# Local attention in a decoder layer: scores of both head groups in PSUM banks of their own, and every engine's order re-dealt

## The reference, cut to what matters

```python
qkv = shift_tokens(x) @ Wqkv                 # 128 -> 3 x 1024, 16 heads of 64
q, k = l2norm(q) * qs, l2norm(k) * ksc       # then rotary tables on both
sim  = q @ k(window and the one before) * 8  # windows of 32 tokens, masked
out  = softmax(sim) @ v
x    = out @ Wo + x
h    = layernorm(shift_tokens(x))
x    = ((h @ W1a + b1a) * gelu(h @ W1g + b1g)) @ W2 + b2 + x
```

## Time and profile before

| | us |
|---|---|
| median of 3 runs | 2246.68 (2245.82 to 2247.02) |
| profiled execution, its own time | 2248.77 |
| span of that profile | 2247.0 |
| TensorE, share of the span busy | 94% |
| VectorE | 82% |
| ScalarE | 74% |
| GpSimd | 74% |

### The profile page before, as it was taken

The page is one execution under the profiler, slowest core; times in us unless marked ns, Lnnn a source line. Parts: engine busy times, 40 slices in busy tenths (PEclk is TensorE's granted clock), DMA queues, the critical chain, the costliest instruction groups (busy, mean ns, idle before and its releaser), DMA issues. The chain is left out here.

```text
span 2247.0 us, 70768 instructions
## 1 busy us (share of the span) xinstructions
PE 2105.5 (94%) x26387; PEld 1439.5 (64%) x26387; DVE 1842.6 (82%) x2689; ACT 1660.0 (74%) x3300; POOL 1654.5 (74%) x1553
## 2 busy tenths in 40 slices
PE   5899869999889999999999999999999999999995
PEld 3555436666646676667676676667667666676764
DVE  4898967777778888888888888888888888888883
ACT  5898845454368788788878878887887887888773
POOL 4677852333378888888888888888888888888881
PEclk8999999999999999999999999999999999999996
DMA  2222220000012223232322322232232222223221
GB/s 77 104 69 67 64 77 1 2 1 1 8 47 77 70 61 79 71 81 61 81 70 59 81 70 76 67 79 72 59 81 70 71 72 74 78 58 82 70 66 45
DMA packets 103501, 140.43 MB, mean 62 GB/s; under 512 B 63376, under 2 KB 64400, under 8 KB 103056
## 3 DMA queue, kind: packets, MB, share of 16 engines
q1 hardware_dynamic: 103440, 139.64, 23.0%
HBM read 56.39 MB, written 1.31 MB: 26 GB/s over the span
## 5 line engine op out<-in xcount | busy, mean ns | idle before, releaser
L1740 PE MATMUL f_psA<-f_W,f_xT 128*128 (+1 forms) x1154 | 603.4, 619 | 7.7 <-ACT f_Vt L1492 3.6
L1630 DVE TENSOR_TENSOR f_m<-f_psA,f_tab 128x1024 f32<-128x1024 f32 x385 | 460.0, 1215 | 78.5 <-ACT f_sq L1474 78.5
L1410 POOL TENSOR_TENSOR f_qkr<-f_qkr,f_rn 128x1024 f32<-128x1024 f32 x192 | 361.4, 1904 | 17.2 <-POOL f_rn L1433 17.2
L1381 POOL TENSOR_TENSOR f_Pr<-f_Pr,f_rden 128x384 f32<-128x384 f32 x384 | 308.1, 835 | 87.2 <-DVE f_rden L1619 87.2
L1474 ACT ACTIVATE f_sq<-f_psA 128x512 f32<-128x512 f32 x385 | 222.2, 590 | 107.0 <-PE f_psA L1740 103.5
L1740 PEld LDWEIGHTS f_psA<-f_W,f_xT 128*128 128x128 f32 x1154 | 192.6, 190 | 131.2 <-issue 90.5
L1606 DVE TENSOR_REDUCE f_mx<-f_psS 128x8 f32<-128x768 f32 x192 | 183.9, 958 | 83.6 <-PE f_psS L1775 83.6
L1400 POOL TENSOR_TENSOR f_qkr<-f_m 128x512 f32<-128x512 f32 x192 | 244.7, 1274 | 7.5 <-DVE f_m L1630 7.5
L1401 POOL TENSOR_TENSOR f_qkr<-f_m 128x512 f32<-128x512 f32 x192 | 246.4, 1283 | 0.0
L795 POOL TENSOR_TENSOR x_Es<-x_E 128x512 f32<-128x512 f32 x64 | 81.4, 1272 | 188.8 <-PE x_psO L1012 127.7
L1661 DVE TENSOR_REDUCE f_ssq<-f_sq 128x32 f32<-128x2048 f32 x96 | 218.5, 2276 | 0.0
(11 more groups left out here) (176 smaller groups left out, 4710.8 us busy)
## 6 DMA issues: line engine op xcount, KB each, us to landing
f_V<-f_Vt SPq DMA_DIRECT2D x96, 384.0 KB, 4.5
f_V<-f_Vt SPq DMA_DIRECT2D x96, 256.0 KB, 3.7
f_W<-in_f_W SPq DMA_DIRECT2D x48, 344.0 KB, 4.6
m_Cb<-m_BC_rows SPq DMA_DIRECT2D x64, 256.0 KB, 3.2
f_W<-in_f_W SPq DMA_DIRECT2D x48, 296.5 KB, 4.2
f_V<-f_Vt SPq DMA_DIRECT2D x48, 128.0 KB, 2.3
f_xsA<-xall SPq DMA_DIRECT2D x98, 32.0 KB
f_xsA<-xall SPq DMA_DIRECT2D x98, 31.8 KB
```

The costliest lines, as they stand in the source:

```text
L1381: pool.tensor_tensor(pv, pv, rv.unsqueeze(3).broadcast_to([P, 2, 2, KEYS]), ALU.mult).then_inc(Pr_ready[g][j], 1)
L1410: pool.tensor_tensor(qv, qv, rv.unsqueeze(3).broadcast_to([P, 2, GH, DH]), ALU.mult).then_inc(qkr_ready[g], 1)
L1630: dve.tensor_tensor(m12[:, j, :, half].rearrange("p m (h d) -> p m h d", d=DH), psA[n % 2][:, :].rearrange("p (h d) -> p h d", d=DH).unsqu ...
L1740: pe.matmul(psA[n % 2][:, :], xT[:, t, :], weights(i, W_QKV + n * 512, 512), start=True, stop=True).then_inc(A_full[n_fill], 1)
```

## The change

PSUM is dealt anew. `psD` is one bank, `psO` is gone, `psX` has two banks. Group 0's scores are in `psX`, group 1's in `psS`. Every tenant of every bank moves accordingly, with the waits that guard them. On TensorE both `scores` calls stand together, group 1 first, and the products with V of both groups behind them; the projection done ahead for the next tile is 2 and not 1; the three gates are in the D slot, at its end, and the three ups at the start of the E slot. ScalarE's, VectorE's, GpSimd's and SP's orders follow: all three GELUs are in the D slot between two table loads; ScalarE's exponentials come as 1, 0; V loads go in front of x1's shifted rows. No arithmetic is added or removed.

```diff
-        psD = [ps(f"f_psD{j}", [P, 512]) for j in range(2)]
+        psD = ps("f_psD", [P, 512])
...
-        psO = ps("f_psO", [P, 4, P])
-        S4 = psS[:, :, 0:GH // 2 * KEYS].rearrange("p a (c k) -> p a c k", k=KEYS)
+        psX = ps("f_psX", [P, 2, 512])
+        project_bank = [psP[:, :], psX[:, 0, :], psA[1][:, :], psA[0][:, :], psA[0][:, :], psA[1][:, :]]
+        S2 = [psX, psS]
+        S4 = [x[:, :, 0:GH // 2 * KEYS].rearrange("p a (c k) -> p a c k", k=KEYS) for x in S2]
...
         def probs_bank(g, half):
-            return psS[:, half, :] if g else (psO[:, :, :].rearrange("p c q -> p (c q)"), psP[:, :])[half]
+            return psX[:, half, :] if g else (psA[0][:, :], psD[:, :])[half]
...
         def qk_bank(g, half):
-            return psS[:, half, :] if g else (psP[:, :], psD[1][:, :])[half]
+            return psS[:, half, :] if g else (psD[:, :], psP[:, :])[half]
...
         def out_bank(g):
-            return psP[:, :].rearrange("p (c q) -> p c q", q=P) if g else psO[:, :, :]
+            return (psP, psA[0])[g][:, :].rearrange("p (c q) -> p c q", q=P)
...
+        def gate_bank(c):
+            return (psP[:, c * T2:(c + 1) * T2], 0) if c < 2 else (psD[:, T2:2 * T2], 1)
+        def a_bank(c):
+            return (psX[:, 1, c * T2:(c + 1) * T2], 0) if c < 2 else (psD[:, T2:2 * T2], 1)
```

SyncE, GpSimd and ScalarE (order inside a slot, new side; waits as before unless shown):

```diff
# SP: shift_in, then
+                if "E" in stages and not (isinstance(i, int) and i > ITERS):
+                    load_up_projection(i - 1)
+                if "A" in stages:
+                    for j in range(2):
+                        sp.wait_ge(A_free[8 + j], u + 1)
+                    for g in range(2):
+                        at_least(sp, O_free[g], u - 1)
+                    (V96 loads, Vtail first where t == 1)
                 if "C" in stages:
                     sp.wait_ge(x1_ready, i * 2 + (t - 1))
                     (xsC loads)
# POOL: rn, scale 1, scale 0, then
+                    normalise_probs(wu, 1, 0)
+                    normalise_probs(wu, 1, 1)
+                    residual_bias(done, i + (t - 2), q)
                     scaled_tables(u + 1, i + t, 1 - t)
-                    for g in range(2):
-                        normalise_probs(wu, g, 0)
-                        normalise_probs(wu, g, 1)
-                    rotate(u, t, 0)
-                    residual_bias(done, i + (t - 2), q)
+                    normalise_probs(wu, 0, 0)
+                    normalise_probs(wu, 0, 1)
                     rotate(u, t, 1)
+                    rotate(u, t, 0)
                     normalise_rows(done, i + (t - 2), q)
# ACT, whole slot, new order
+ square 3; evacuate_qk(1,0); square 2; evacuate_qk(0,1); evacuate_qk(0,0); square 1; evacuate_v(0)
+ evacuate_qk(1,1); square 0; evacuate_tokens; evacuate_probs (1,1) (1,0) (0,1) (0,0); evacuate_v(1)
+ lnq; rn0; lnC; rstdC; evacuate_out(1); evacuate_out(0); exponentials(1); D: xnT; exponentials(0)
+ D: preload GELU; gate_gelu(2); gate_gelu(0); gate_gelu(1); preload LN_EXP
# DVE, whole slot, new order
+ E: gated 0, 1, 2; table_products 3, 2; statistics; table_products 1, 0; squares' sum
+ maximum(1); less_maximum(1); maximum(0); less_maximum(0); denominators(1); x1
+ reciprocals(1); denominators(0); reciprocals(0); E: x2
```

TensorE, whole slot, new order with the waits that are new:

```diff
+ E: wait S_free[0]; up(0); up(1); wait ge_ready (first GELU); up(2)
+ wait x1_ready (slot before); project 3
+ transpose_qk(1)
+ (E: wait h2_ready, ge_ready; D: P_free[0][1], O_free[0] of the slot before) transpose_qk(0)
+ wait S_free[0]; D: wait x2_done; project 1
+ wait A_free[3]; project 4;  wait A_free[4]; transpose_tokens;  wait A_free[5]; project 0;  wait A_free[2]; project 5
+ (wait S_free[0], A_free[1], E: h01_ready) transpose_probs(1);  (wait A_free[8], xT_ready) transpose_probs(0)
-                    if g == 1:
-                        pe.wait_ge(S_free[0], v + 1)
-                    elif "C" in stages:
+                    if g == 0 and "C" in stages:
                         pe.wait_ge(P_free[1][0], wu + 1)
                         pe.wait_ge(P_free[1][1], wu + 1)
+ scores(1); scores(0)
+ (wait P_free[1][*], P_free[0][0]) times_v(1);  (wait P_free[0][*], A_free[0]) times_v(0)
+ wait A_free[9]; project 2 of the next tile
+ D: wait hatC_ready, O_free[0]; hatC transposes;  wait O_free[0], O_free[1]; W_O
+ E: wait S_free[0]; W_2
+ D: wait xnT_ready, w1_loaded, P_free[0][1]; gate(2); gate(0); gate(1)
```

More of the change, by code:

```diff
@@ L1334, in slot @@
                         sp.dma_start(xsC[0:1, 1, 64:D], x1[P - 1:P, 0, 64:D]).then_inc(xsC_ready[t], 16)
[L1335 to L1349, removed]
                 if "A" in stages and t == 1 and not is_first(i):
@@ L1486, in evacuate_v @@
                     act.wait_ge(A_full[8 + j], u + 1)
-                    if j == 1 and not is_first(i):
+                    if j == 0 and not is_first(i):
                         act.wait_ge(V96_ready[t], i * 32)
@@ L1516, in slot @@
                 if "A" in stages:
-                    square(u, 0)
                     square(u, 3)
@@ L1520, in slot @@
                     evacuate_qk(1, 0)
+                if "A" in stages:
+                    square(u, 2)
+                if "B" in stages:
+                    evacuate_qk(0, 1)
                     evacuate_qk(0, 0)
+                if "A" in stages:
+                    square(u, 1)
+                    evacuate_v(0)
+                if "B" in stages:
                     evacuate_qk(1, 1)
                 if "A" in stages:
-                    square(u, 2)
+                    square(u, 0)
                     evacuate_tokens(u + 1, 1 - t)
-                if "B" in stages:
-                    evacuate_qk(0, 1)
+                if "C" in stages:
+                    evacuate_probs(1, 1)
+                    evacuate_probs(1, 0)
+                    evacuate_probs(0, 1)
+                    evacuate_probs(0, 0)
                 if "A" in stages:
                     evacuate_v(1)
[L1530 to L1543, removed]
                     act.wait_ge(ssq_ready, u + 1)
                     act.activation(lnq[:, :], ssq[:, :], ACT.Ln, bias=consts[:, 0:1], scale=SSQ_SCALE).then_inc(lnq_done, 1)
-                    square(u + 1, 1)
+                    at_least(act, rn_ready, u)
+                    act.wait_ge(lnq_done, u + 1)
+                    act.activation(rn0[:, :], lnq[:, :], ACT.Exp, bias=consts[:, 1:2], scale=-0.5).then_inc(rn0_ready, 1)
                 if "c" in stages:
@@ L1574, in slot @@
                     gate_gelu(2)
+                    gate_gelu(0)
+                    gate_gelu(1)
+                    act.preload_act_table_set(LN_EXP)
+                if stages == "CcE":
+                    final_deviation(0)
             evacuate_tokens(0, 0)
-            square(0, 1)
             slot(0, 0, "A")
@@ L1726, in _ @@
             slot(ITERS + 1, 0, "cD")
+            final_rows(1)
             slot(ITERS + 1, 1, "E")
@@ L1768, in scores @@
                             r = slice(par * HQ, par * HQ + HQ)
-                            pe.matmul(S4[0:HQ, par, :, 0:WIN], same_row[r, 0:HQ], outside[r, :].rearrange("p (c k) -> p c k", k=WIN), start=False, stop=False, skip_group_check=True)
+                            pe.matmul(S4[g][0:HQ, par, :, 0:WIN], same_row[r, 0:HQ], outside[r, :].rearrange("p (c k) -> p c k", k=WIN), start=False, stop=False, skip_group_check=True)
                     for c in range(4):
@@ L1823, in transpose_qk @@
                     else:
-                        at_least(pe, O_free[1], v - 1)
-                        if t == 0 and not (isinstance(i, int) and i < 2):
-                            pe.wait_ge(h01_ready, (i - 1) * 2)
-                        at_least(pe, A_free[5], v)
+                        if "E" in stages:
+                            pe.wait_ge(h2_ready, i)
+                            pe.wait_ge(ge_ready, (i - 1) * 3)
+                        else:
+                            at_least(pe, P_free[0][1], wu)
+                            at_least(pe, O_free[0], wu)
+                        if isinstance(i, int) and "A" in stages:
+                            pe.wait_ge(A_free[0], u)
                     alone(pe, passed)
@@ L1836, in transpose_qk, with gate, up @@
                                 ins.then_inc(A_full[4 + 2 * g + half], 1)
-                def w1(n, c, full):
-                    ins = pe.matmul(bank_of(c)[0][0:FC[c], :], W1[:, n * FF + c * P:n * FF + c * P + FC[c]], xnT[:, :], start=True, stop=True)
+                def gate(c):
+                    ins = pe.matmul(gate_bank(c)[0][0:FC[c], :], W1[:, FF + c * P:FF + c * P + FC[c]], xnT[:, :], start=True, stop=True)
                     if c > 0:
-                        ins.then_inc(full[bank_of(c)[1]], 1)
+                        ins.then_inc(gate_full[gate_bank(c)[1]], 1)
+                def up(c):
+                    ins = pe.matmul(a_bank(c)[0][0:FC[c], :], W1[:, c * P:c * P + FC[c]], xnT[:, :], start=True, stop=True)
+                    if c > 0:
```

(23 more changed lines are left out.)

206 lines of the change are left out of this document (104 added, 102 removed).

## The result

The changed kernel takes 2221.78 us (median of 4 runs, 2220.61 to 2222.71), against 2246.25 us of the kernel before beside it: a ratio of 0.9892, 95% interval [0.9875, 0.9909], or 24.5 us less. The forecast was 2213, in a range of 2195 to 2250. The profiled execution is 2221.15 us with a span of 2219.4, 27.6 us less than the span before.

What follows compares the result with a forecast made beforehand. TensorE's own order was taken as the bound: 1.09 us gained an iteration, less 0.20 and 0.15 for late releases, gives 0.74; times 46 iterations, 34 us. Forecast 2213 us, range 2195 to 2250.

Steps and rivals of the forecast that it cites:

- recorded sum: TensorE's new order laid out from timeline starts: slots of 15.3 and 16.45, 31.75 us an iteration instead of 32.84.
- The stall: TensorE, second scores waiting for VectorE's subtraction on shared banks: 0.40 us a slot lost, 0.80 an iteration to be gained.
- changes of operand shape: TensorE, switches between narrow and wide operands: 0.1 to 0.2 us lost a change; the gain beyond the stalls.
- late releases: TensorE waiting for other engines: 0.20 us an iteration for probability copies, 0.15 for ties such as the GELU tail.
- The GELU tail: ScalarE, subtraction 0 to the odd slot's square 3: no slack, lateness goes into the period; slower, 2270, chance 0.10.
- The rival that it would take all: No change: near ties among nine releases an iteration take the whole gain, 2240 to 2250 us, chance 0.09.
- The shifted rows: V loads ahead of x1's rows delay VectorE's statistics and product 1 in even slots; slower, 2270, chance 0.07.
- Edges: Two slots before the loop and four behind, re-ordered with the same instructions: -2 to +3 us, taken as 0.

Runs made afterwards that it cites:

- square 2 ahead: Changed kernel with square 2 of the next tile behind exponential 1, table product 2 before 3, projection 0 before 4; 2197.23 us, ratio 0.9779.
- scores apart: Changed kernel with scores 0 behind the products with V instead of beside scores 1, no wait added; 2310.62 us, ratio 1.0283.
- the load out of the tail: Changed kernel with the second table load moved from behind the last GELU to the odd slot, behind the token copy; 2238.70 us, ratio 0.9963.
- the run with the old order: Changed kernel with x1's shifted rows issued in front of the V loads again, the W1 load staying ahead; 2221.99 us, ratio 0.9893.

## Why the prediction was right, point by point

**What bounds.** TensorE's own order did, and the starts in the timeline gave its price. But the recorded sum has a slip: the odd slot's terms (no hatC, no gates, ups 1.38, two scores 0.05 longer each, W_2 1.34) add up to 16.55 and not to 16.45, the 0.10 for the longer scores having been left out. So the placed order takes 31.86 us an iteration and not 31.75, and gains 0.98 and not 1.09. From the starts in the timelines (us; "changed" is the changed kernel, "ahead" the one with square 2 ahead):

| stretch | placed, even / odd | changed, even / odd | ahead, even / odd |
|---|---|---|---|
| projection 3, q/k transposes | 2.17 / 2.17 | 2.09 / 2.14 | 2.08 / 2.18 |
| projection 1 up to the probabilities | 3.91 / 3.91 | 3.99 / 4.19 | 3.91 / 3.74 |
| probabilities up to W_O | 6.17 / 5.97 | 6.27 / 5.96 | 6.30 / 6.02 |
| W_O; even: gates; odd: W_2, ups | 3.06 / 4.50 | 3.18 / 4.43 | 3.18 / 4.41 |
| slot | 15.31 / 16.55 | 15.53 / 16.72 | 15.47 / 16.35 |

The kernel with square 2 ahead is within 0.07 us of the placed sum, and a little under it. The terms stand in their sum, not one by one: single ones are off by up to 0.1 both ways (projection 1 takes 0.96 and not 0.86, the token transpose 0.11 and not 0.17, W_O in even slots 1.88 to 1.89 and not 1.78), and that they cancel is luck.

**The stall.** Put at 0.80 us an iteration. The waits are gone from the trace, and the run that puts the wait back, into the kernel with the scores apart, pays 0.63 us and 30.6 us of time for it. The part for changes of operand shape, 0.29 as recorded and 0.98 - 0.80 = 0.18 with the sum put right, was not tried alone.

**Who releases TensorE.** The forecast took 0.20 + 0.15 = 0.35 us an iteration for late releases. Against the sum put right, 32.25 - 31.86 = 0.39 came, so its size was nearly right; its places were not. At scores 0 and the products with V, where 0.20 stood, no such gap shows (0.95 to 1.00 apart): they are just in time, as the run with the scores apart shows. The loss is in front of the probabilities. Table product 3 was placed to release projection 4's bank at 2.9; with 1.23 us for one product it does so at about 3.0 in even slots (1519.11 + 1.23 - 1517.32) and 3.2 in odd ones (1503.84 + 1.23 - 1501.90), and projection 4 starts at 3.16 and 3.22 where 3.0 was placed. The rest of the difference between the slots is at the probabilities, 1.18 against 0.99 behind projection 5. Square 2 ahead takes 0.45 us out of that stretch of the odd slot.

**The loop and the sum.** 46 x 0.74 = 34 was forecast, 46 x 0.597 = 27.4 came. Of the 0.15 us an iteration too few, 7 us, the slip in the sum is 0.10, and the forecast without it would have been 46 x 0.63 = 29 us, 2218. The rest to the 24.5 us between medians is how the profiled executions stand to them.

**Rivals.** The GELU tail did decide a part of it, in the place and in the way described, but a small one: with the load out of the tail projection 4 of the odd slot gains 0.09 us and the probabilities behind it nothing, while the even slot, with no tail in front, has the same wait at projection 4. The rival that it would take all was near even so: half a microsecond more in the tail, one copy, ends at 2244.5 us. The shifted rows were not late, as the run with the old order shows. But their cover is thin. The timeline of VectorE behind the loop in the changed kernel, to be held against the earlier trace rows:

```profile
2161.48 0.29 DVE L1680 TENSOR_TENSOR f_x<-f_psA,xall 128x128 f32<-128x128 f32 x1 [0.56 <-PE f_psA L1921]
2166.31 0.29 DVE L1660 BATCH_NORM_STATS2 f_statC<-f_xsC 128x6 f32<-128x128 f32 x1 [2.67 <-DMA f_xsC<-f_x]
```

Here the rows land 2166.31 - 2161.77 = 4.54 us after x1's end, 0.35 later than before, and in the loop's even slot they are asked for 1521.38 - 1516.73 = 4.65 us after it. If they take as long there, 0.1 us of cover is left, where 0.4 was placed.

**Edges.** Put at 0; 27.6 - 27.4 = 0.2 us.

## What to carry to other kernels

When one engine is full, lay its new order out from the starts in its timeline and not from busy times; that sum held within 0.07 us of 32. Add it up twice: a slip of 0.10 us in it was 4.6 us of the time here, half of what the forecast was off by. Then go through every release it waits for, add the time from a release to the restart (0.05 to 0.36 us here), and treat a tie as a loss: of two engines that meet with no slack, the period pays whatever either slips. The remedy was not to shorten the tail but to put work that is ready early (a square, a table product, another projection) in front of the piece that waits for it, and ScalarE's idle gaps are no free place when what stands behind them is needed just in time.

## What the runs showed that I had not expected

An in-order engine's lateness doesn't stay with the release it was measured on: with table product 3 covered, the same 0.5 us of ScalarE work still cost 0.34 us an iteration, through the copies queued behind square 3. A projection that starts after a wait also costs 0.10 us more than the wait, in its own longer record. And the time from a release to TensorE's restart is not one number. Projection 4 starts about 0.05 us after table product 3's end in the changed kernel's odd slot (1503.84 + 1.23 = 1505.07 to 1505.12). The probabilities there, which have one wait more (for the gated products), start 0.36 us after table product 1's end (1506.64 + 1.23 = 1507.87 to 1508.23), in the even slot 0.25 (1521.92 + 1.23 = 1523.15 to 1523.40). Whether the additional wait is the cause was not tried.
